# Local attention: the scalar engine's output copy moved from the middle of a chunk's exponentials to their front

## The reference, cut to what matters

```python
# B = 4 images, T = 1024 tokens here, 16 query heads of size 64 share one key/value head
q = _rmsnorm(_rope(q), q_norm_w)
k = _rmsnorm(_rope(k), k_norm_w)
mask = (cols <= rows) & (rows - cols <= WINDOW)        # WINDOW = 128
scores = jnp.einsum('bqgtd,bqgsd->bqgts', q, k) * scale
scores = jnp.where(mask[None, None, None], scores, NEG)
attn = jax.nn.softmax(scores, axis=-1)
out = jnp.einsum('bqgts,bqgsd->bqgtd', attn, v)
out = out.transpose(0, 3, 1, 2, 4).reshape(Bx, Tx, QPG * N_KV * D_HEAD)
return out @ wo.T
```

## Time and profile before

| | us |
|---|---|
| Three runs | 914.52, 912.0, 903.77 |
| Their median | 912.0 |
| The profiled execution: its own time | 905.44 |
| The profiled execution: span in the trace | 902.8 |

### The profile page before, as it was taken

How to read it: one execution, slowest core, us unless ns; L and a number is a source line. 1 busy time by engine, 2 the same in 40 slices (tenths; PEclk the granted TensorE clock), 3 DMA queues, 4 the chain that set the end, 5 groups by cost and what they waited for, 6 DMA issues and landing times. The chain is left out here.

```text
span 902.8 us, 21152 instructions
## 1 busy us (share of the span) xinstructions
PE 739.3 (82%) x8196; PEld 484.5 (54%) x8196; DVE 607.1 (67%) x1209; ACT 448.7 (50%) x1405; POOL 429.4 (48%) x556
## 2 busy tenths in 40 slices
PE   6699999899998989988789979987899986405880
PEld 6243776426774447763267734773577753303660
DVE  0478887588885988876878836676577759512870
ACT  0024999127994359972299925312666650101100
POOL 0655666274662656643656612662033230472675
PEclk9889999999999999999999998997999997556755
DMA  7353000170000710001200000008000004017000
GB/s 253 118 204 73 3 3 3 46 219 14 2 4 1 233 45 3 3 3 29 62 2 3 3 1 1 1 3 110 8 3 2 2 2 129 27 44 129 9 18 14
DMA packets 60008, 41.30 MB, mean 46 GB/s; under 512 B 51760, under 2 KB 57389, under 8 KB 59124
## 3 DMA queue, kind: packets, MB, share of 16 engines
q1 hardware_dynamic: 57462, 33.03, 14.5%
q10 hardware_dynamic: 144, 4.19, 1.2%
q0 software_dynamic: 2304, 2.74, 0.9%
HBM read 25.44 MB, written 7.15 MB: 36 GB/s over the span
## 5 line engine op out<-in xcount | busy, mean ns | idle before, releaser
L795 ACT ACTIVATE work<-ps,small,rq 128x160 f32<-128x160 f32 x512 | 242.8, 487 | 31.9 <-DVE small L741 31.4
L774 POOL TENSOR_TENSOR work<-work,small 128x512 f32<-128x512 f32 x128 | 133.1, 1040 | 123.9 <-DVE small L758 123.9
L738 DVE TENSOR_REDUCE ps<-ps 128x4 f32<-128x640 f32 x128 | 106.5, 832 | 40.5 <-PE ps L648 39.2
L795 ACT ACTIVATION_READ_ACCUMULATOR work<-ps,small,rq 128x1 f32 x512 | 105.3, 206 | 0.0
L648 PE MATMUL ps<-kT,big 64*128 64x160 f32 x1024 | 97.8, 311 | 0.0
L750 DVE COPY pT<-ps 128x640 f32<-128x640 f32 x116 | 95.5, 823 | 0.5 <-issue 0.5
L683 PE MATMUL ps<-pT,vwin 128*64 128x128 f32 x1024 | 84.2, 282 | 9.7 <-ACT big L783 2.4
L273 PE MATMUL ps<-xT,s_proj_w 64*128 64x512 f32 x288 | 78.6, 663 | 12.6 <-PEq L213 7.5
L608 POOL TENSOR_TENSOR big<-prod 128x1024 f32<-128x1024 f32 x28 | 65.8, 2361 | 27.4 <-DVE prod L575 27.2
L648 PEld LDWEIGHTS ps<-kT,big 64*128 64x128 f32 x1024 | 76.1, 191 | 0.1
L683 PEld LDWEIGHTS ps<-pT,vwin 128*64 128x64 f32 x1024 | 56.7, 136 | 23.6 <-issue 17.6
(11 more groups left out here) (284 smaller groups left out, 1425.8 us busy)
## 6 DMA issues: line engine op xcount, KB each, us to landing
xb<-in_x SPq DMA_DIRECT2D x3, 4096.0 KB, 14.0
xb<-in_x ACTq DMA_DIRECT2D x1, 4096.0 KB, 18.0
vrem<-hl SPq DMA_DIRECT2D x64, 64.0 KB, 2.1
sent_rows<-empty_row SPq DMA_DIRECT2D x8, 325.0 KB, 9.9
s_proj_w<-in_proj_w SPq DMA_DIRECT2D x1, 1536.0 KB, 6.1
big<-sent_rows SPq DMA_DIRECT2D x5, 264.0 KB, 5.2
big<-sent_rows SPq DMA_DIRECT2D x5, 256.0 KB, 4.6
xb<-in_ffn_w SPq DMA_DIRECT2D x1, 1028.0 KB, 4.6
```

What stands on the lines that cost most here:

```text
L738: ch.step(v.tensor_reduce(row_max(c), ps[:, s_banks(c), 0:2 * SPAN].rearrange("p e (h k) -> p e h k", h=2), X, ALU.max))
L774: g.tensor_tensor(probs[:, c % 3, :, 0:P], probs[:, c % 3, :, 0:P], bc(small[:, c % 4, 3, :], P), ALU.mult)
L795: nc.scalar.activation(probs[:, c % 3, q, :], bank[2 * (c % 2) + e][:, SPAN * hh:SPAN * hh + SPAN], ACT.Exp, bias=small[:, c % 4, 1, q:q + ...
```

## The change

One condition moves. `outputs(c - 4)` is issued in front of the first exponential of chunk `c` (`q == 0`) where it was issued between the second and the third (`q == 2`). It holds for chunks 4 to 31 of each image, so 28 copies per image and 112 in all. Nothing is added or removed.

```diff
@@ -789,7 +789,7 @@
                     if c >= 3:
                         a.wait_ge(S["transposed"], c - 2)
                     for q in range(NQ):
-                        if q == 2 and c >= 4:
+                        if q == 0 and c >= 4:
                             outputs(c - 4)
                         e, hh = divmod(q, 2)
                         nc.scalar.activation(probs[:, c % 3, q, :],
```

## The result

| | before | changed |
|---|---|---|
| Median, us (4 runs each) | 912.84 | 923.72 |
| Lowest to highest | 903.77 to 914.52 | 918.44 to 927.94 |
| Profiled execution, its own time | 905.44 | 924.73 |
| Its span | 902.8 | 922.8 |

The ratio is 1.0156, 95% interval 1.0109 to 1.0204: **1.6% slower, some 14 us** (10 to 19). The two medians of the table are 10.9 us apart, inside that interval. That is the forecast direction, and the median lies in the range of 907 to 926, but the cost is twice the 6.6 us that were forecast.

What follows compares the result with a forecast made beforehand. A loop over four engines, not ACT alone, was taken to bound the kernel at 4.37 us a pair. At 4.48, 13 x 0.11 + 0.21 = 1.64 us per image, 6.6 for four, gave 918.6 us, range 907 to 926.

Steps and rivals of the forecast that it cites:

- the loop: Old steady cycle of scores, maxima, bias, two exponentials, copy, values product, scores; said to set the pace, 4.37 us a pair.
- the second term of the sum: In the new cycle, values product's start to the start of the copy that waits for it: 0.51 us.
- each wake of the copy costs more: Rival: the moved copy's three waits cost another 0.05 us per chunk, 5.2 us in all, up to 926.6; chance 0.10.
- terms 1 to 4: New cycle over two steps: 1.65 or 1.72, 0.51, 2.24 and 0.06 us, summing to 4.46 or 4.53 a pair.
- the tail: End of each image: the last four exponentials start later, shifting the first copy there by 0.21 to 0.28 us.
- The other terms: Step start to last products 1.65 or 1.72, copy's start to fourth accumulator read's end 2.24, then to scores 0.06 us.
- The chosen 1.65 over 1.72: Two readings of step start to last values products; the pair was taken nearer the shorter one's sum, at 4.48 us.
- The rival of a falling clock: TensorE's clock drops in the steady steps: about 1 us on each of 112 steps, over 100 us; chance 0.01.
- Faster: Rival: values product starts under 1.56 us behind its step's start, ACT sets 4.22 a pair, 904.2 us; chance 0.07.
- No change: Rival: ACT is the full engine and its work stays, 912.0 us on the median; chance 0.08.
- The wait of 0.1 to 0.2 us in nearly all copies: Confirming sign: a wait of that size before the moved copy, put down to the values product, in nearly all 112.
- waits near nothing: Refuting sign: if the copies of outputs had hardly any wait before them, the forecast was wrong.

## Why the prediction was right in direction and short by half in size

**What bounds the kernel before: right.** Leaving out an exponential that isn't on the loop changed nothing, and putting one more on the loop cost its full 0.46 us.

**The step that failed is the second term of the sum, "L680's start to the start of the copy that waits for it: 0.51"**. That row is a copy with one wait. In the loop the moved copy has three, as the instruction rows of the change say, and it took 0.60. The text knew the difference and put it into a rival, "each wake of the copy costs more", with 0.05 us per chunk and a chance of 0.10. It was 0.09 per copy. The loop of terms 1 to 4 spans two steps and holds this term once, and so does the tail: 4.56 a pair for 4.48, and 0.31 for 0.21. The rival counted its extra twice, 0.05 a chunk as 0.10 a pair, which the prediction's own sum doesn't bear out. Priced by 0.60, the sum would have been (13 x 0.19 + 0.31) x 4 = 11.1 us, against 11.2 by image 0 and 11.3 to 11.5 by all four. That is 4.5 of the 7 to 8 us that the forecast of 6.6 lacked. Of the others, 1.8 are the low clock in tails, and the rest lies inside the interval of 10 to 19.

The other terms held within 0.01 us: 1.66, 2.25, 0.06. The chosen 1.65 over 1.72 was right. Between the two steps of a pair the lengths are 133.63 - 131.27 = 2.36 and 2.21, not both 2.24 as the text had it.

**The tail** grew by the term and, in five of 16, by a low clock. The rival of a falling clock was given 0.01 for a drop over the whole loop, which didn't come (1.00 in the loop). In the tail it did, and neither the price nor the place was in the text.

**The rivals.** *Faster*: L680 would have had to start under 1.56 us behind the step's start; it starts 1.66 behind. What this rival wanted is had with the copy one exponential later, where it is ready in time and its bank is free in time: 4.28 a pair, near to the 4.22 that ACT's row of work allowed. *No change*: refuted by four orders of the same work with four different times.

The Trainium skill ("PSUM — Partial Sum Buffer", Summary: rules for kernel authors) says to evacuate promptly and gives the tightness of PSUM's space as its reason. As a rule for time it isn't borne out here: the earliest copy is 1.6% slower than the one two exponentials later. The place one exponential behind the earliest is the best of the four.

The Trainium skill's rule to optimize the engine of highest occupancy first ("Perfetto Trace Analysis", Identifying the Most-Contended Engine) doesn't hold for the kernel before: 0.46 us a chunk could be taken from the full ACT, and the time stayed as it was.

**What would show it.** L683's wait for the copy in the loop is gone, no exponential of the loop waits for its bias in the rows shown, the first exponential is 0.28 behind the copy (0.26 forecast) and 133.81 - 131.27 = 2.54 behind the scores (2.4). The wait of 0.1 to 0.2 us in nearly all copies is not what the profile shows. It labels 22 waits (15.1 us), and 12 of them (10.3 us) are in the tails, so only 10 of the loops' 112 copies have one. By the prediction's own sign, waits near nothing, this would have spoken against it. The label is missing because an accumulator read is drawn up to 133.36 + 0.22 = 133.58 while the copy starts at 133.53. The time is there, but smaller than forecast: from the last exponential's start to the copy it is 133.53 - 132.99 = 0.54, where two neighbours without a wait are 0.46 apart, so 0.08.

**Left open:** why a wait that is already met costs 0.02 to 0.06 us, and whether every semaphore costs alike; what picks the value of the last stages; what brings the low clock in the tail in some executions and not in others.

## What to carry to other kernels

Where an in-order queue holds an instruction that both waits and is waited for, draw the loop over all engines and put it where its input is surely done and its output is not yet wanted. An engine that is full in the profile need not set the pace: leave a piece of its work out and see. Here that place is one exponential wide, half a microsecond, with a costlier place on either side. Read a latency from an instruction that carries the same waits as the one you move, and where a moved instruction stands in front of a group, place it ahead of the waits that belong to the group: here that took the pair from 4.56 to 4.48 us.

## What the runs showed of the hardware that was not expected

- From the start of the product to the start of the ACT copy that waits for it: 0.51 to 0.52 us with one semaphore wait on the copy, 0.57 to 0.58 with two, 0.60 with three, though the added semaphores were signalled earlier.
- The row of an exponential is 0.52 us long with the copy behind the first exponential and 0.48 to 0.49 in the other orders, but the starts of two neighbours are 0.46 to 0.48 us apart in the first and 0.46 in the others. The longer row isn't an exponential slower by as much. No run tells why it is longer.
- The clock fell to a mean of 0.56 over 3.9 us in a tail of one execution and stayed at 1.00 in the same tail of another, with gaps of 0.9 us ahead of it in both. Such a fall cost 1.2 us in six of the seven tails that had one.
